# Two TensorE transpositions per turn replaced by SBUF-to-SBUF block transfers and DVE 32x32 block transpositions

## What is computed

```python
logits = jnp.einsum('bsh,he->bse', x, router_w) + router_b + load_balancer
rw, sel = jax.lax.top_k(logits, K)                     # K = 2 of 4
rw = jax.nn.softmax(rw, axis=-1)
e0 = jax.nn.silu(x @ sw_w1) * (x @ sw_w3) @ sw_w2
e1 = jax.nn.gelu(sym @ me_c1w + me_c1b, approximate=False) @ me_c2w + me_c2b
e2 = h2 @ ce_gen_w + ce_gen_b                          # h2: two layer norms with a relu block
e3 = jax.nn.gelu(x @ ml_w1 + ml_b1, approximate=False) @ ml_w2 + ml_b2
...
xn = _layernorm(x, axis=-1)
x = x + attention(xn) + (rw[..., None] * gathered).sum(axis=2)
```

## Time and profile before

| | us |
|---|---|
| median of 3 runs (467.31 to 467.6) | 467.48 |
| the profiled execution, its own time | 467.11 |
| its span from first to last instruction | 465.3 |
| PE busy | 455.2 (98%) |
| DVE busy | 390.9 (84%) |
| ACT busy | 270.8 (58%) |
| POOL busy | 249.9 (54%) |

### The profile page before, as it was taken

How to read it: one execution, slowest core, us unless ns; L and a number is a source line. 1 busy time by engine, 2 the same in 40 slices (tenths; PEclk the granted TensorE clock), 3 DMA queues, 4 the chain that set the end, 5 groups by cost and what they waited for, 6 DMA issues and landing times.

```text
span 465.3 us, 9571 instructions
## 1 busy us (share of the span) xinstructions
PE 455.2 (98%) x2908; PEld 381.7 (82%) x2908; DVE 390.9 (84%) x1297; ACT 270.8 (58%) x534; POOL 249.9 (54%) x366
## 2 busy tenths in 40 slices
PE   5999999999999999999999999999999999999996
PEld 4778898888978878898888978878888888978876
DVE  5888879889798888979889798888979889797887
ACT  4855828466482845828466482845828466482841
POOL 3874726457272664726457272664726457272361
PEclk9999999999999999999999999999999999999999
DMA  7400010100101001010100101001010100100001
GB/s 266 23 24 2 0 47 1 46 1 1 47 0 45 0 2 43 0 45 0 45 0 0 45 0 45 0 3 42 0 45 0 45 0 0 45 1 23 2 6 41
DMA packets 18802, 11.43 MB, mean 25 GB/s; under 512 B 1152, under 2 KB 18272, under 8 KB 18784
## 3 DMA queue, kind: packets, MB, share of 16 engines
q1 hardware_dynamic: 18496, 11.20, 9.1%
q10 hardware_dynamic: 288, 0.01, 0.0%
HBM read 6.80 MB, written 4.19 MB: 24 GB/s over the span
## 4 chain that ended last, share of the span: by engine, by line
PE 98%; DMA 1%; DVE 1%; ACT 0%; issue 0%; SPq 0%; DVEq 0%
PE S L1035 14%; PE S L1037 13%; PE S L1036 13%; PE EX L976 12%; PE EX L996 6%; PE EX L1004 4%; PE S L1123 3%; PE S L1119 3%; PE S L1118 3%; PE ATT L1107 3%; PE TR L941 2%; PE S L1129 2%; PE S L1130 2%; PE S L1131 2%; PE TR L1075 2%; PE S L1050 2%
## 5 line engine op out<-in xcount | busy, mean ns | idle before, releaser
L1035 PE MATMUL S<-xh,WH 128*128 128x512 f32 x224 | 98.7, 441 | 0.0
L1037 PE MATMUL S<-xh,WL 128*128 128x512 f32 x224 | 88.4, 395 | 0.0
L1036 PE MATMUL S<-xl,WH 128*128 128x512 f32 x224 | 88.1, 393 | 0.0
L448 POOL TENSOR_TENSOR hid3l<-hid,hid3h 128x512 fp32r<-128x512 f32 x64 | 80.3, 1283 | 0.0
L406 POOL TENSOR_TENSOR veps_x<-mv_x,eps 128x4 f32<-128x4 f32 x16 | 3.2, 199 | 118.9 <-DVE mv_x L602 118.9
L976 PE MATMUL EX<-scaled,hid 128*128 128x128 f32 x512 | 59.8, 275 | 0.0
L580 ACT ACTIVATE hid<-S,me_b 128x512 f32<-128x512 f32 x32 | 22.0, 688 | 63.8 <-PE S L1037 63.6
L976 PEld LDWEIGHTS EX<-scaled,hid 128*128 128x128 f32 x512 | 58.4, 192 | 0.0
L1035 PEld LDWEIGHTS S<-xh,WH 128*128 128x128 f32 x224 | 42.2, 189 | 16.6 <-issue 3.6
L704 DVE SCALAR_TENSOR_TENSOR OUT<-EX,coef,OUT 128x128 f32<-128x128 f32 x188 | 52.6, 342 | 0.7
L763 DVE SCALAR_TENSOR_TENSOR gate<-th,S 128x512 f32<-128x512 f32 x64 | 43.9, 686 | 8.2 <-ACT th L527 7.5
(11 more groups left out here) (182 smaller groups left out, 1078.2 us busy)
## 6 DMA issues: line engine op xcount, KB each, us to landing
X<-x SPq DMA_DIRECT2D x16, 256.0 KB, 2.9
out<-OUT SPq DMA_DIRECT2D x15, 256.0 KB, 2.4
W<-weights SPq DMA_DIRECT2D x1, 768.0 KB, 8.1
W<-weights SPq DMA_DIRECT2D x1, 512.0 KB, 5.6
W<-weights SPq DMA_DIRECT2D x1, 384.5 KB, 6.6
W<-weights SPq DMA_DIRECT2D x1, 384.0 KB, 6.1
out<-OUT SPq DMA_DIRECT2D x2, 128.0 KB, 1.8
W<-weights SPq DMA_DIRECT2D x1, 192.5 KB, 4.3
```

The source lines that it names most:

```text
L448: pool.tensor_tensor(hid3l[:, j, :], hid[3][:, j, :], hid3h[:, j, :], ALU.subtract) \
L1035: pe.matmul(bank[:, :], wh, hi, start=True, stop=False)
L1036: pe.matmul(bank[:, :], wh, lo, start=False, stop=False)
L1037: pe.matmul(bank[:, :], wl, hi, start=False, stop=True).then_inc(unit_ready, 1)
```

## The change

- In each turn but the last, SP copies `xn` of the next group into a new buffer `xb` by 16 transfers within SBUF (`swap_x`). Each moves a block of 32 partitions by four times 32 elements: block row i, block column j of a tile goes to block row j, block column i, for all four tiles at once. Inside a 32x32 block nothing is turned yet.
- DVE then turns all 32x32 blocks of `xb` by one instruction of 128x512 into `TR` (`turn_next`). It stands behind `silu(2)`; in turn 0 behind L861. PE's `turn_x` is left only for group 0.
- In each turn but the first, SP does the same for `e3T` of the group before, into `e3b` (`swap_e3`), and DVE turns it into `e3t` in SBUF, behind `silu(3)`, and mixes it from there, ahead of `expert2_add`. So expert 3 is mixed one turn later. In the last turn PE's `expert3` and the old mix stay, `expert3` now behind the transposition of `u`.
- ACT may write `e3T` only when DVE has turned the blocks of the group before (`ex_ready[3]`).
- On SP the store moves behind both swaps and the load.

```diff
+            def swap(dst, src, done):
+                for i in range(P // B):
+                    for j in range(P // B):
+                        sp.dma_start(dst[j * B:(j + 1) * B, :, i * B:(i + 1) * B],
+                                     src[i * B:(i + 1) * B, :, j * B:(j + 1) * B]).then_inc(done, DMA_INC)
+            def swap_x(g):
+                sp.wait_ge(x_normed, g.count(NT, NT))
+                swap(xb, xn, x_swapped)
+            def swap_e3(g):
+                b = g.bank("e3")
+                sp.wait_ge(released[b], g.uses_before("e3") + 1)
+                swap(e3b, e3T, e3_swapped)
...
             def turn(g, first, last):
                 if not first:
-                    store(g.prev())
+                    swap_e3(g.prev())
+                if not last:
+                    swap_x(g.next())
                 if two_more(g):
                     sp.wait_ge(att_added, g.count(1, 1))
                     load_x(Group(g.pair, g.off + 2))
+                if not first:
+                    store(g.prev())
...
+                wait(act, ex_ready[3], g.count(1, 0))
                 e3, free = unit("e3")
...
             def expert0(g):
-                mix(g, 0, ex_taken[3])
+                mix(g, 0, bias1_added)
...
+            def turn_next(g):
+                dve.wait_ge(route_step, g.count(ROUTE_STEPS, ROUTE_STEPS - 1))
+                dve.wait_ge(h2_ready, g.count(1, 1))
+                dve.wait_ge(x_swapped, g.count(SWAPS * DMA_INC, SWAPS * DMA_INC))
+                dve.transpose(TR[:, :], xb[:, :, :].rearrange("p t n -> p (t n)")).then_inc(x_turned, 1)
...
                 silu(2)
+                if not first and not last:
+                    turn_next(g)
                 dve.wait_ge(tlean_ready, g.count(1, 1))
...
                 silu(3)
...
+                if not first:
+                    wait(dve, ex_taken[3], g.prev().count(1, 0))
+                    dve.wait_ge(e3_swapped, g.prev().count(SWAPS * DMA_INC, SWAPS * DMA_INC))
+                    dve.transpose(e3t[:, :, :].rearrange("p t n -> p (t n)"), e3b[:, :, :].rearrange("p t n -> p (t n)")) \
+                        .then_inc(ex_ready[3], 1)
+                if not first:
+                    mix(g.prev(), 3, ex_taken[1], src=e3t)
                 if not first:
                     expert2_add(g.prev())
...
+                if first:
+                    turn_next(g)
                 if not last:
                     x_low(g.next())
-                mix(g, 3, bias1_added)
                 if two_more(g):
                     x_moments(Group(g.pair, g.off + 2))
+                if last:
+                    mix(g, 3, bias1_added)
...
             def last_experts(g):
+                expert3(g)
...
-                pe.wait_ge(route_step, g.count(ROUTE_STEPS, ROUTE_STEPS - 1))
-                pe.wait_ge(h2_ready, g.count(1, 1))
-                if not last:
-                    turn_x(g.next())
-                expert3(g)
                 if not last:
```

More of the change, by code:

```diff
@@ L74 @@
 TOKW = LOGW + 2 * C
+B = 32
 BEHIND = NT - 1
+SWAPS = NT * NT
 ZEROTH = BEHIND * P - 1
@@ L168, in build @@
         xn = sb("xn", [P, NT, P])
+        xb = sb("xb", [P, NT, P])
         xh = [sb(f"xh{k}", [P, T], F32R) for k in range(2)]
@@ L187, in build @@
         hid3l = sb("hid3l", [P, 4, T], F32R)
-        e3T = sb("e3T", [P, T])
+        e3T = sb("e3T", [P, NT, P])
+        e3b = sb("e3b", [P, NT, P])
+        e3t = sb("e3t", [P, NT, P])
         h2 = sb("h2", [P, T])
@@ L250, in build @@
         x_turned = sem("x_turned")
+        x_swapped = sem("x_swapped")
         x_high = sem("x_high")
@@ L282, in build @@
         hid3_low = sem("hid3_low")
+        e3_swapped = sem("e3_swapped")
         u_turned = sem("u_turned")
@@ L573, in turn @@
                 half_gate(3)
+                wait(act, ex_ready[3], g.count(1, 0))
                 e3, free = unit("e3")
-                act.activation(e3T[:, :], e3[:, :], ACT.Identity, bias=vec("ml_b2")).then_inc(free, 1)
+                act.activation(e3T[:, :, :].rearrange("p t n -> p (t n)"), e3[:, :], ACT.Identity, bias=vec("ml_b2")).then_inc(free, 1)
                 if not last:
@@ L697, in fold_last, with mix @@
                                        VEC[:, VECS.index("me_c1b0"):VECS.index("me_c1b0") + 2], ALU.add))
-            def mix(g, e, added, count=None):
+            def mix(g, e, added, count=None, src=None):
                 dve.wait_ge(ex_ready[e], g.count(1, 1))
@@ L703, in mix @@
                 for t in range(NT):
-                    ins = dve.scalar_tensor_tensor(out=OUT[g.par][:, t, :], in0=EX[EX_BANK[e]][:, t, :],
+                    ins = dve.scalar_tensor_tensor(out=OUT[g.par][:, t, :], in0=(src or EX[EX_BANK[e]])[:, t, :],
                                                    scalar=coef[g.par][:, t, e:e + 1], in1=OUT[g.par][:, t, :],
@@ L720, in expert2_add @@
                 dve.wait_ge(ex_taken[2], g.count(1, 1))
-                dve.wait_ge(ex_taken[1], g.count(1, 1))
+                dve.wait_ge(ex_taken[3], g.count(1, 1))
                 for t in range(NT):
@@ L980, in expert3 @@
             def expert3(g):
-                wait(pe, ex_taken[1], g.count(1, 0))
+                pe.wait_ge(ex_taken[1], g.prev().count(1, 1))
                 b = g.bank("e3")
@@ L985, in expert3 @@
                 for t in range(NT):
-                    ins = pe.transpose(EX[EX_BANK[3]][:, t, :], e3T[:, t * P:(t + 1) * P], ident[:, :])
+                    ins = pe.transpose(EX[EX_BANK[3]][:, t, :], e3T[:, t, :], ident[:, :])
                 ins.then_inc(ex_ready[3], 1)
             def expert1(g):
-                pe.wait_ge(ex_taken[3], g.count(1, 1))
+                wait(pe, ex_taken[1], g.count(1, 0))
                 b = g.bank("m1")
```

## The result

| | before | after |
|---|---|---|
| median, us (four runs each) | 467.54 | 473.69 |
| lowest to highest | 467.31 to 468.57 | 473.05 to 474.63 |
| span of the profiled execution | 465.3 | 472.1 |

The ratio is 1.0125 with an interval of 1.0097 to 1.0154. The forecast was 456.5 in a range of 454.5 to 465.0: wrong in sign, and outside its range. What happened is rival (d), SP as the bound, at a smaller price than the 491 it was given.

The account below looks back on a forecast made before the run. PE was taken as the bound, with DVE only about 2.5 us short of it. From 467.11, 15 x (27.90 - 27.10) = 12.0 off and 0.97 on made 456.1; the median, 0.37 above, 456.5, range 454.5 to 465.

Parts of the forecast that it names:

- rival (d): SP becomes the bound: issues at 0.64 make its loop 29.5 us a turn, 491 us in all; chance 10%.
- SP and the swaps: SP's queue: 32 added issues at 0.45 us each make a loop of 23.4, hidden under a turn of 27.1.
- The bound of 0.565: Issue price in us from which SP's loop would bound the turn; the old turn is reached at 0.59.
- The doubt about transfers under 64 KB: On the swaps: a documentation page says descriptors dominate such transfers, which speaks against sixteen transfers of 16 KB for one group.
- 9.0 + 32 issues: Length of the loop through SP: store, landing and the DVE steps up to the signal take 9.0 us, plus the issues.
- near ties: Loops of PE, DVE and DVE with POOL end within 0.2 us; 0.07 added to PE's 27.03 makes 27.10 a turn.
- (b): Rival on DVE: block transpositions dearer than a one-pass step, at 0.85 and 0.9 us, giving 461 us; chance 14%.
- (c): Rival on DVE: block transpositions take two passes, 0.45 us more on each, giving 469.7 us, slower; chance 4%.
- DVE's loop: DVE's queue in a turn: 25.31 us without its waits, 1.56 added, 26.87 in all, 0.16 under PE's 27.03.
- ACT's wait: ACT's e3T waits for DVE's transposition of the group before: 0.8 us late, covered by later work.
- The signs named for the profile: What would show the forecast: turn of 27.0 to 27.2, issues at 0.4 to 0.5, no DVE wait for a DMA.
- The tail: Turn 15: DVE's added expert 3 work makes u 1.0 late and the later mix costs 0.97 us.

Follow-up runs that it names:

- x_only: The kernel after with expert 3 done as in the kernel before, so only x is swapped, 16 issues a turn: 461.81 us, ratio 0.9882.
- e3_only: The kernel after with turn_x kept on PE, so only expert 3 is swapped, 16 issues a turn: 462.29 us, ratio 0.9901.
- e3_first: The kernel after with only SP's order changed: the swap of e3 goes ahead of the store, in its own turn: 458.52 us, ratio 0.9803.
- bounce: The kernel after, same order, with each swap going through memory, 5 issues instead of 16: 456.81 us, ratio 0.9753.
- dose4: The kernel after with four more transfers of the swap's form on SP each turn, into a buffer nobody reads: 511.26 us.
- the two kernels with the old ends: e3_first, and bounce in e3_first's order, each with group 1's x and expert 3 of groups 14 and 15 on PE: 457.66 and 455.63 us.
- coef_late: The kernel before with DVE's step for coef moved from between silu(2) and silu(3) to behind silu(3): 467.24 us.

## Why the prediction was wrong, and where it was right

**The step that failed** is the price of an issue in "SP and the swaps". I had three kinds of rows and took 0.45, near the middle-turn loads and stores at 0.38 to 0.39. Both of those have memory on one side. The only rows with SBUF on both sides, mask at 0.59 and 0.64 ahead of reach, I set aside because "the engines were full then"; reach itself, three issues in 2.54 or 0.85 each, was dearer still and isn't in the working. The runs show the contrary: a median of 0.60 with a spacing of 0.65 in the middle turns, and 0.59 to 0.67 for eight forms in the middle of the kernel before, where SP has nothing else to do. Of the 17.8 us between the forecast span (11.0 less) and the measured one (6.8 more), the 14 turns that this loop now sets make 4.36 + 11.2 = 15.6. The bound of 0.565 in the same paragraph was the place to see that a choice between 0.45 and 0.64 decided the sign; with 10% for the row that was of the right kind the chances were wrong too. The doubt about transfers under 64 KB pointed at the swap for another reason, bandwidth. A swap's 16 KB land 1.8 us behind their issue's start, where 256 KB take 2.4, but that isn't what bound.

**The loop itself was right, its constant too large.** At 0.645 the forecast's 9.0 + 32 issues gives 29.6, and the turn is 28.2. The landing was added behind the last issue, but counts from its start, and is 1.8 rather than 2.4: 1.2 less. coef was carried at 0.74, and is 0.19 behind turn_next: 0.55 less. The pass from one loop of two turns to the next adds 0.35 every second turn. That makes 29.6 - 1.2 - 0.55 + 0.2 = 28.0.

**PE: right.** 0.43 and 0.44 came off in x_only and e3_only, and the turn is 27.04 to 27.05 where SP doesn't bound. The 0.07 for near ties wasn't seen there.

**DVE: right in its parts.** The block transpositions in the list by line of the kernel after:

```profile
L780 DVE STREAM_TRANSPOSE TR<-xb 128x512 f32<-128x512 f32 x15 | 10.9, 727 | 23.6 <-DMA xb<-xn 23.6
L894 DVE STREAM_TRANSPOSE e3t<-e3b 128x512 f32<-128x512 f32 x15 | 10.6, 705 | 0.0
```

As steps they cost 0.64 (230.51 to 231.15) and 0.74 (232.73 to 233.47), with 0.65 and 0.72 forecast, and mix to expert2_add is 1.25 for 1.23. Rivals (b) and (c) fall. The sum of DVE's loop was still 0.55 too high, because turn_next took the place of coef's hold behind POOL: from the last of silu(2) to silu(3) it is 1.42 in e3_first (223.00 to 224.42) and 1.34 before (225.24 to 226.58), so that a whole transposition cost 0.08. That error lay hidden, as DVE bounds in neither kernel.

**ACT's wait: right.** e3T waits for the DVE in all 15 turns, 4.8 us on average (72.2 / 15). Before, ACT already waited 2.9 there, for PE, so e3T is some 1.9 late where 0.8 was forecast, since DVE is late itself. In bounce the wait is 48.0 / 15 = 3.2, 0.3 more than before. The loop that bounds the kernel after doesn't run through e3T, and in bounce the turn is PE's.

**The signs named for the profile.** Held: no idle time of DVE ahead of u, 0 to 0.2 ahead of stats_u in all turns but the last (0.48), transpositions of 0.66 to 0.75, PE in the tail waiting for u (0.5 us), POOL's wait ahead of the norm of n gone in the middle turns. The waits of DVE and POOL are gone for another reason than the one forecast, though: DVE comes late from its swap, and in bounce, where it doesn't, it waits for PE again. Not held: a turn of 27.0 to 27.2 (28.23), issues at 0.4 to 0.5, no wait for a DMA.

**Start and tail: too small.** The forecast took its gain off 15 turns, and turn 0 gives none. bounce shows it best: with both sets of products gone PE waits 0.66 ahead of expert 0, for a step of DVE that reads PE's EX bank (me_b, only in turn 0) and stands behind coef, which takes 2.26 there, and silu(3).

```profile
PE EX L1029 <- DVE me_b L730: 0.7, 1, 0.7
```

Expert 0 of turn 0 starts at 35.23 there and at 35.19 before. So 0.80 of the forecast was never there. The 0.37 of the kernel after isn't the swap's work either: turn_next of turn 0 waits 0.74 for its swap and x_low 0.65 for take_x, but u of turn 0, ahead of both, is 0.35 late already (35.40 against 35.05), and from there to stats_u it is 5.76 against 5.74.

The tail was given 0.97. Expert 3's mix comes 461.50 - 436.36 = 25.14 behind the last turn's stats_u, where it was 455.24 - 431.63 = 23.61: 1.5 more. 0.49 of that is a stall of DVE that the profile puts down to no one, and without it the forecast term would stand:

```profile
439.49 0.38 DVE L833 BATCH_NORM_AGGREGATE mv_c<-stats_c 128x2 f32<-128x6 f32 x4 [0.49 <-issue]
```

It is there in dose4, e3_first and bounce too, and neither before nor in the two kernels with the old ends. Its cause is open. The other 0.54 of the tail's 2.07 stand behind the mix, at the last store, whose two issues take 1.13 us where they took 0.89; why is open too.

e3_first is 2.0 us above the forecast by the medians. In its profiled execution, 459.76 and 3.7 above the 456.1 of the sum, the start is 1.56 late and turn 0 lacks its 0.80 (2.4 together, 1.43 of it the late start named above), the 14 turns give 0.5 less than forecast (27.15 each, with the waits for the swap), and the tail takes 0.9 more.

## What to carry to other kernels

Price a DMA issue by a row with the same two ends, not by the nearest in time, and multiply by the count on that queue before thinking of bytes: 32 issues of 0.65 made 20.9 us of a 28 us turn. When such a term decides the sign, write down the value at which it does, and give the rival the weight of the best row, not of the wish. And look where a store waits: one wait for a late result ahead of long issues closes a loop that the same issues in another order don't have, and that was 15 us here. No run put part of the issues on another engine's queue.

## What the runs showed of the hardware

- An issue on SP in a middle turn took 0.33 to 0.44 us for a load or a store in runs of 512 bytes and more, 0.59 to 0.67 within SBUF in all eight forms, and 0.63 from SBUF to memory in runs of 128 bytes. The swap's sixteen, back to back within SBUF, start 0.65 apart, and each lands 1.8 us from its issue's start.
- A block transposition of 128x512 in float32 took 0.70 us from SBUF to SBUF and 0.73 to PSUM (means of 15 each).
- The hold of DVE behind POOL is written as busy time: coef, 128x16, took 2.25 us in turn 0 before, ending at 32.51 with POOL's hidl at 32.48, and 0.17 with POOL out of the way (coef_late). A new DVE step put ahead of such a held one is nearly free: 0.08 us for a transposition of 0.64 in e3_first.
